# Second-layer expert weights laid out with two slots on the partitions, in a one-core ViT block with a soft mixture of experts

## What is computed

```python
y = jnp.einsum('btd,bst->bsd', xn, dispatch_w)          # 16 x 64 x 192
y = jnp.einsum('sio,bsi->bso', fc1_weight, y) + fc1_bias # 64 slots, 192 -> 768
y = jax.nn.gelu(y, approximate=False)
y = jnp.einsum('sio,bsi->bso', fc2_weight, y) + fc2_bias # 64 slots, 768 -> 192
out = jnp.einsum('bsd,bst->btd', y, combine_w)
```

## Time and profile before

| | |
|---|---|
| three executions | 221.20, 221.53, 221.94 us; median 221.53 |
| the profiled execution | 220.9 us |
| its span, first to last instruction | 219.1 us |
| busy: TensorE matmul / weight load / VectorE / ScalarE / GpSimd | 193.7 / 127.4 / 63.9 / 64.2 / 45.2 us |
| DMA | 80.68 MB in 17827 packets, mean 368 GB/s |
| packets under 8 KB | 13774 |

### The profile page before, as it was taken

One profiled execution on the slowest core, in us unless ns is written; L12 is line 12 of the kernel. 1 busy time (PEld: TensorE's weight loads), 2 busy tenths in 40 slices (PEclk: granted clock), 3 DMA queues, 4 the chain that ended last, 5 costly groups with the idle time before them and its releaser, 6 DMA issues.

```text
span 219.1 us, 4816 instructions
## 1 busy us (share of the span) xinstructions
PE 193.7 (88%) x2048; PEld 127.4 (58%) x2048; DVE 63.9 (29%) x153; ACT 64.2 (29%) x161; POOL 45.2 (21%) x91
## 2 busy tenths in 40 slices
PE   6699999999999998999999999839996789766994
PEld 6699876466667556556464655424564346532662
DVE  1556563579884631121110211100210011000213
ACT  2552433345565364150322304101300121010300
POOL 7701068575464400101001010100010000000000
PEclk9999999999999999999999999996999999997999
DMA  6999999999999499999999999999999999999912
GB/s 170 288 234 408 416 412 388 310 363 363 403 368 429 168 379 416 344 431 427 405 412 419 426 409 409 421 422 416 411 420 421 413 412 415 426 417 406 400 52 81
DMA packets 17827, 80.68 MB, mean 368 GB/s; under 512 B 2697, under 2 KB 4398, under 8 KB 13774
## 3 DMA queue, kind: packets, MB, share of 16 engines
q1 hardware_dynamic: 17806, 80.38, 94.6%
HBM read 79.46 MB, written 0.91 MB: 367 GB/s over the span
## 4 chain that ended last, share of the span: by engine, by line
DMA 48%; PE 41%; DVE 4%; ACT 2%; issue 2%; POOL 1%; SPq 0%; DVEq 0%; ACTq 0%; POOLq 0%
DMA ring<-in_L_ffn_fc_weight_dram 39%; PE ps L1285 9%; PE ps L1312 7%; PE ps L917 6%; PE ps L1259 4%; DMA value_store<-ring 3%; DMA ring<-value_store 3%; DMA ring<-in_x_dram 3%; PE ps L942 2%; PE ps L1137 2%; PE ps L1248 2%; PE ps L1298 2%; PE ps L911 1%; PE ps L1028 1%; PE ps L1041 1%
## 5 line engine op out<-in xcount | busy, mean ns | idle before, releaser
L1285 PE MATMUL ps<-ring,qkvT 128*32 128x384 f32 x384 | 43.4, 596 | 12.4 <-DMA ring<-in_L_ffn_fc_weight_dram 12.0
L1312 PE MATMUL ps<-ring,x_space 128*32 128x192 f32 x768 | 34.5, 328 | 4.3 <-DMA ring<-in_L_ffn_fc_weight_dram 3.6
L1285 PEld LDWEIGHTS ps<-ring,qkvT 128*32 128x32 f32 x384 | 12.9, 117 | 34.2 <-issue 28.6
L888 DVE TENSOR_TENSOR region_p<-ps,b1T 128x384 f32<-128x384 f32 x16 | 8.8, 557 | 81.4 <-PE ps L1298 81.4
L1312 PEld LDWEIGHTS ps<-ring,x_space 128*32 128x32 f32 x768 | 23.7, 110 | 14.3 <-DMA ring<-in_L_ffn_fc_weight_dram 5.3
L646 ACT ACTIVATE x_space<-ps,row_scale 128x384 f32<-128x384 f32 x16 | 15.1, 941 | 48.8 <-PE ps L1285 48.8
L1259 PE MATMUL ps<-projT,soft_space 128*108 128x192 f32 (+1 forms) x96 | 19.1, 329 | 0.4 <-ACT projT L683 0.4
L911 PEld LDWEIGHTS ps<-ident 128*128 128x128 f32 x116 | 15.5, 212 | 6.4 <-issue 4.6
L911 PE MATMUL ps<-ident 128*128 128x128 f32 x116 | 17.5, 304 | 1.8 <-POOL neg_half L384 1.8
L469 POOL COPY bias_space<-ident 64x128 f32<-64x128 f32 x8 | 2.2, 286 | 81.0 <-PE ps L1248 81.0
L683 ACT COPY projT<-ps 128x192 f32<-128x192 f32 x8 | 2.5, 318 | 52.7 <-PE ps L1312 52.7
(11 more groups left out here) (139 smaller groups left out, 218.3 us busy)
## 6 DMA issues: line engine op xcount, KB each, us to landing
ring<-in_L_ffn_fc_weight_dram SPq DMA_DIRECT2D x31, 2304.0 KB, 24.6
ring<-in_L_ffn_fc_weight_dram SPq DMA_DIRECT2D x3, 768.0 KB, 5.6
ring<-in_x_dram SPq DMA_DIRECT2D x2, 864.0 KB, 8.0
ring<-in_L_tok_W_proj_dram SPq DMA_DIRECT2D x1, 576.0 KB, 7.2
ring<-in_L_attn_w_qkv_dram SPq DMA_DIRECT2D x1, 432.0 KB, 10.6
out_dram<-h SPq DMA_DIRECT2D x2, 162.0 KB
value_store<-ring SPq DMA_DIRECT2D x1, 258.2 KB
ring<-value_store SPq DMA_DIRECT2D x3, 86.1 KB
```

The costliest lines, as they stand in the source:

```text
L888: dve.tensor_tensor(pre[:, pr, :, :].rearrange("p c (k b) -> p c k b", b=B), ps[:, 2 + pr, 0:384].rearrange("p (c k b) -> p c k b", c=3, b=B),
L1285: mm = pe.matmul(ps[32 * k:32 * k + 32, pr, 0:FF // 2], y_group[:, g % 2, j, 2 * pr + qq, :], w[:, qq, j, :, 3 * hf:3 * hf + 3], start=(j ...
L1312: mm = pe.matmul(ps[32 * q:32 * q + 32, 4, 0:D], gact[:, q // 2, k, 32 * l:32 * l + 32], w[:, q, c, :], start=(l == 0 and c == 0), stop=(l ...
```

## The change

Second-layer units take the layout of the first-layer ones. A unit now holds four *neighbouring* slots (two pairs q), and a partition holds twelve rows of 192 floats of one slot in one run of 9216 B: partitions 0 to 63 have the first slot of a pair (64 x 12 = 768 rows), 64 to 127 the second. To fit this, the hidden rows and the first bias must arrive with the slot's parity u on the partition half, so the three transposes of a turn become, for each of six column blocks, two matmuls against columns picked from the identity (`ident` seen as k, u, b), one into each half of the bank; the bias turn becomes 24 matmuls. GELU works on one half of the partitions with 384 elements. The second layer of unit 2 + l needs only the hidden rows of pair half l, and writes its own bank (4 or 3); its two column strips for even and odd c give two halves that are added: ScalarE copies one half (`keep_part`), VectorE adds the other (`fold`). `combine` waits for both. The first layer's moving columns are picked as 6 of 12 neighbouring floats instead of 3 of 6. The fillers write bank 2 instead of 3.

```diff
-        fc2_view = fc2_w.rearrange("(q l) (p c) d -> l p q (c d)", l=2, p=128)
+        fc2_view = fc2_w.rearrange("s f d -> (s f) d").rearrange("(q p c) d -> p q (c d)", p=128, c=2 * FC)
+        SECOND = (4, 3)
...
-                if u < 2:
-                    dst = ring[:, slot, :].rearrange("p (q n) -> p q n", q=2)
-                    src = fc1_view[:, 4 * g + 2 * u:4 * g + 2 * u + 2, :]
-                else:
-                    dst = ring[:, slot, :].rearrange("p (q n) -> p q n", q=4)
-                    src = fc2_view[u - 2][:, 4 * g:4 * g + 4, :]
-                sp.dma_start(dst, src).then_inc(unit_in[slot], 16)
+                pair = 4 * g + 2 * (u % 2)
+                src = (fc1_view if u < 2 else fc2_view)[:, pair:pair + 2, :]
+                sp.dma_start(ring[:, slot, :].rearrange("p (q n) -> p q n", q=2), src).then_inc(unit_in[slot], 16)
...
-                act.activation(gact[:, pr, :, :].rearrange("p k (l n) -> p k l n", l=2)[:, :, 0, 0:B],
-                               pre[:, pr, :, :].rearrange("p c (k l b) -> p (c k) l b", l=2, b=B)[:, :, 0, :],
-                               ACT.Gelu).then_inc(gact_ready, 1)
...
+                for u in range(2):
+                    half = slice(64 * u, 64 * u + 64)
+                    act.activation(gact[half, pr, :, B * u:B * u + B],
+                                   pre[half, pr, :, :].rearrange("p c (k b) -> p (c k) b", b=B),
+                                   ACT.Gelu).then_inc(gact_ready, 1)
+
+            def keep_part(g, l):
+
+                part = slice(64 * (1 - l), 64 * (1 - l) + 64)
+                act.wait_ge(units_used, g * UNITS + 3 + l)
+                act.copy(y2[64 * l:64 * l + 64, g % 2, :], ps[part, SECOND[l], 0:D]).then_inc(part_kept, 1)
...
-                act.wait_ge(units_used, (g + 1) * UNITS)
-                act.copy(y2[:, g % 2, :], ps[:, 4, 0:D]).then_inc(y2_ready, 1)
+                keep_part(g, 0)
+                keep_part(g, 1)
...
+            def fold(g, l):
+
+                part = slice(64 * l, 64 * l + 64)
+                dve.wait_ge(part_kept, 2 * g + l + 1)
+                dve.tensor_tensor(y2[part, g % 2, :], ps[part, SECOND[l], 0:D], y2[part, g % 2, :],
+                                  ALU.add).then_inc(y2_ready, 1)
...
+                fold(g, 0)
                 keep_mix(g, g % 2)
+                fold(g, 1)
...
-                b1v = b1_raw[0:S, :].rearrange("s (p c) -> s c p", c=FC)
-                for c in range(FC):
-                    mm = pe.transpose(ps[:, 3, c * S:(c + 1) * S], b1v[:, c, :], ident[0:S, 0:S])
+                b1v = b1_raw[0:S, :].rearrange("s (p c) -> s c p", c=2 * FC)
+                for c in range(2 * FC):
+                    for u in range(2):
+                        mm = pe.matmul(ps[64 * u:64 * u + 64, 3, c * S // 2:(c + 1) * S // 2], b1v[:, c, :],
+                                       ident[0:S, u:S:2], start=True, stop=True)
...
-                    pe.wait_ge(y2_ready, g + 1)
+                    pe.wait_ge(y2_ready, 2 * g + 2)
...
-                w = ring[:, slot, :].rearrange("p (q j n c) -> p q j n c", q=2, j=3, c=FC)
+                w = ring[:, slot, :].rearrange("p (q j n c) -> p q j n c", q=2, j=3, c=2 * FC)
...
-                                           w[:, qq, j, :, 3 * hf:3 * hf + 3],
+                                           w[:, qq, j, :, FC * hf:FC * hf + FC],
...
-                for c in range(3):
-                    mm = pe.transpose(ps[:, 2 + pr, c * 128:(c + 1) * 128], hid[:, pr, c, :], ident[:, :])
+                for c in range(FC):
+                    for u in range(2):
+                        mm = pe.matmul(ps[64 * u:64 * u + 64, 2 + pr, c * 64:(c + 1) * 64], hid[:, pr, c, :],
+                                       ident[:, :].rearrange("p (k u b) -> p u k b", u=2, b=B)[:, u, :, :],
+                                       start=True, stop=True)
...
-                if l == 0:
-                    pe.wait_ge(gact_ready, g * 4 + 4)
-                    earlier(pe, y2_ready, g)
...
+                pe.wait_ge(gact_ready, g * 4 + 2 * l + 2)
+                earlier(pe, y2_ready, 2 * g)
+                w = ring[:, slot, :].rearrange("p (q c d) -> p q c d", q=2, c=2 * FC)
+                for c in range(2 * FC):
+                    for q in range(2):
+                        k = 2 * (c % 2) + q
+                        mm = pe.matmul(ps[32 * k:32 * k + 32, SECOND[l], 0:D],
+                                       gact[:, l, (c % FC) * 4 + 2 * q + c // FC, :], w[:, q, c, :],
+                                       start=(c < 2), stop=(c >= 2 * FC - 2), tile_position=(0, 32 * k))
```

More of the change, by code:

```diff
@@ L667, in _ @@
                     for hf in range(2):
-                        act.copy(b1T[:, :, :, 2 * hf:2 * hf + 2],
-                                 ps[:, 3, hf * 3 * S:(hf + 1) * 3 * S].rearrange("p (c q l) -> p c q l", c=3, l=2)
-                                 ).then_inc(b1_kept, 1)
+                        act.copy(b1T[:, :, :, hf], ps[:, 3, hf * 3 * S:(hf + 1) * 3 * S]
+                                 .rearrange("p (c q) -> p c q", c=6)).then_inc(b1_kept, 1)
                 keep_hidden(g, 1)
@@ L1304, in second_layer @@
                 pe.wait_ge(unit_in[slot], 16 * ((g * UNITS + 2 + l) // RING) + 16)
-                if l == 0:
-                    pe.wait_ge(gact_ready, g * 4 + 4)
-                    earlier(pe, y2_ready, g)
-                w = ring[:, slot, :].rearrange("p (q c d) -> p q c d", q=4, c=FC)
-                for c in range(FC):
-                    for q in range(4):
-                        k = (c % 3) * 4 + 2 * (q % 2) + c // 3
-                        mm = pe.matmul(ps[32 * q:32 * q + 32, 4, 0:D], gact[:, q // 2, k, 32 * l:32 * l + 32],
-                                       w[:, q, c, :], start=(l == 0 and c == 0), stop=(l == 1 and c == FC - 1),
-                                       tile_position=(0, 32 * q))
+                pe.wait_ge(gact_ready, g * 4 + 2 * l + 2)
[7 more added lines that the diff above has]
+                                       start=(c < 2), stop=(c >= 2 * FC - 2), tile_position=(0, 32 * k))
                 mm.then_inc(units_used, 1)
```

27 lines of the change are left out of this document (12 added, 15 removed).

## The result

| | before | after |
|---|---|---|
| median of 10 executions each | 221.88 us | 223.94 us (222.77 to 226.34) |
| ratio after / before | | 1.0081, interval 1.0045 to 1.0117 |
| the profiled execution | 220.9 us | 225.61 us |
| its span | 219.1 us | 223.9 us |
| DMA packets | 17827 | 13734 |

The profiled execution of after lies 1.7 us above its median.

A forecast was written before the change was run, and what follows sets the result against it. DMA and TensorE were taken to share the end. Unit 2 +0.3 us and eleven late units -1.65 made the last landing -1.35; with the addition's +0.4, -0.95 us: 220.6 us on the median, 8 in 10 from 219.7 to 222.4.

The forecast's parts named there:

- What bounds the kernel: DMA and TensorE both set the end, unit 31's start at 210.95 us; either one alone becoming earlier wins nothing.
- Long runs: Second-layer loads in 9216 B runs: 0.15 us less for each of 11 late units, -1.65 us.
- the early part: Two second-layer units with long runs, ahead of the stored values and their reload: -0.3 us from 44 us on.
- Bias turn: Ahead of unit 2: 24 pairs at 70 ns, 1.68 us instead of 0.89, +0.79 us (+0.57 to +1.34).
- unit 10's issue: Early in the weight queue: this issue moves by +0.03 us and stays hidden.
- rival A: Unit 29 again at 1.2 GHz, TensorE ends last, the DMA's gain is wasted: +0.1 us, 221.6 us; chance 0.22.
- Hidden turns: Each turn of hidden rows, now 12 pairs at 70 ns: 0.84 us instead of 0.38, +0.46 us.
- rival B: In the turns, the two array halves run one after the other: +2.8 us, 224.3 us; chance 0.06, milder form 0.08.
- First layer: Moving rows read in 24 B runs: gain of 0 to 0.46 us a unit, half taken, 0.23.
- Rival D: First layer unchanged, so unit 2 is 0.46 us later: -0.5 us, 221.0 us; chance 0.12.
- TensorE at the end: From unit 29's landing at 198.5 us, TensorE at full clock is free at 209.1, before unit 31's landing.
- Fold: After the last unit, VectorE's addition of the two halves lies on the path: +0.4 us.

The follow-up runs named there:

- e7: After, with the first bias gathered beforehand by GpSimd into neighbouring floats and without the last group's fillers ahead of unit 31: 221.55 us, ratio to before 0.9948.
- e10: After, with the first bias gathered beforehand by GpSimd into neighbouring floats, all fillers kept: 221.74 us, ratio to before 0.9946.
- e1: Before, with only the second-layer loads changed to runs of 9216 B (weights in wrong order, same work): 219.93 us, ratio to before 0.9914.
- e6: After, with 26 filler instructions instead of 10 ahead of unit 29 in the last group: median 226.27 us.
- e9: Before, with second-layer loads in 9216 B runs and first-layer columns picked as 6 of 12 floats: 219.60 us, ratio to before 0.9885.
- e3: After, with the bias turn's 48 instructions reading neighbouring floats (wrong bias values, same work): 222.47 us in one execution.
- e2: After, with the bias turn as in before, six transposes (bias values in wrong places): 220.26 us, ratio to before 0.9924.
- e8: Before, with only the first layer's moving columns picked as 6 of 12 floats instead of 3 of 6: 220.34 us in one execution.
- e11: After, with the first bias gathered by GpSimd and hidden rows turned by three transposes again (wrong row order): 220.85 us, ratio to before 0.9946.
- e5: After, without the ten filler instructions ahead of unit 31 in the last group: 223.67 us, ratio to before 1.0023.
- e4: After, with the bias turn moved ahead of the values' matmuls: 228.05 us, ratio to before 1.0025.

## Why the prediction was wrong

**The sum against the profiled execution.** Unit 31 was forecast for 209.6 and started at 215.30, 5.7 us later. Up to unit 2 that is 3.4 us, in the main 1.7 from the bias turn (3.35 us instead of 1.68), 2.1 because the first unit started 1.83 us late instead of 0.3 early, and -0.5 because the first layer gained its whole 0.96. From unit 2 to the landing of unit 31 it is another 1.0, and 1.25 is TensorE coming behind that landing. The bias turn is the part that the change brings and that the experiments remove: with it at 1.52 us, near its forecast price, e7 and e10 lie 1.2 us below before, where the forecast was 0.95.

**What bounds the kernel.** Right in part: both bounds are close together at the end, but "if either one alone becomes earlier, nothing is won" isn't so. e1 changed nothing but the loads, and unit 31 started 1.28 us earlier, since unit 29's shorter wait left it the full clock. Unit 31 has no DMA wait in after, 1.54 us in e7 and 0.26 in e6.

**Long runs.** Right in mechanism: 1.65 + 0.3 had been predicted, and e1 alone gave 1.9. That the size fits so well is in part luck. The 0.3 for the early part isn't borne out (e9), and in the profiles e1 wins only 0.93 us between unit 2 (84.65) and unit 31 (209.67), where before has 85.00 and 210.95. The Trainium skill, page "DMA: Bandwidth & Descriptors", section "Why small descriptors are slow", would make the gain 1% by the estimate in the prediction; the trace has 2% (411 to 420 GB/s), so it doesn't agree here.

**Bias turn.** This is the step that failed. I priced its 24 pairs at 70 ns, from rows whose weights lie side by side, and carried "may cost more" only as an upper end of +1.34 us. It measured +2.46: 3.35 us, 140 ns a pair. e3 shows that neighbouring floats bring it to 63 ns, e2 that the old six transposes bring the time to 0.9924. The earlier trace rows had a price that comes near. The old bias turn, which read its weights 24 B apart, took 0.89 us for 6 x 128 weight columns, 1.16 ns a column. The new one loads 24 x 128 = 3072 columns (each pair reads its 64 columns twice, once for each half), which makes 3.6 us at that price. I divided the row by the wrong thing: by instructions, to see how many there would be, instead of by columns read. Even so that row could not have told that the distance is what costs: the hidden turn of the earlier trace rows, whose columns lie side by side, took 0.38 us for 3 x 128 columns, 0.99 ns a column. The distance as the cause is shown by e3 and by the gathered bias.

The Trainium skill, page "SBUF — State Buffer", section "Specifications (TRN2)", says that a 16-byte line needs two hits or more for full bandwidth. I had used that rule for the first layer alone. It speaks of any read, and the weights of the bias turn get one hit a line. e3 and e8 agree with it in direction, 63 against 140 ns and 2.07 against 2.55 us.

**Where the delay goes.** I had unit 10's issue moved by 0.03 us and hidden. With the bias turn at its real price, unit 1 ends 3.3 us later. Unit 10's issue is no longer hidden, and the queue runs dry a second time: 346 GB/s over 80 to 96 us in after and 349 in e6, against 394 in before, 395 in e10 and 413 in e2. The 1.8 us of the queue lost there are about the bias turn's excess. The whole kernels differ by more: after lies 3.5 us above e2, whose turn is 2.46 us shorter, and 3.0 above e10, whose turn is 1.8 shorter. Both excesses, 1.0 and 1.2 us, are as large as the uncertainty. What the rest would be, if there is one, isn't shown; rival A and the clock at 70 us are candidates.

**Hidden turns.** Right: 0.85 us measured (206.61 to 207.46) for 0.84 predicted, 70 ns a pair. Two ahead of unit 2 with the activation make +0.33 us (10.19 in e2 less 9.86 in e9), where 0.46 - 0.18 = 0.28 had been predicted. The halves do overlap; rival B fell.

**First layer.** Half of 0.46 had been taken, and the whole came: 2.55 to 2.07. Rival D fell, and the rule of that page of the Trainium skill gave the right size. It is the one term of the sum that was too pessimistic.

**TensorE at the end.** Rival A, which I gave 0.22, is what the profile shows: unit 29 at the low clock (3.72 us), 12.34 us from its start to unit 31, and no wait there. I argued against it that waits of that size don't always cost the clock. That is true and was no reason to set the case aside. With about 2.0 us of idle time ahead of unit 29, the profiles of before, after, e2, e3, e9 and e11 have the low clock and those of e5 and e7 the full one. In after's profile A cost 1.25 us of its own: unit 31 would otherwise have started at its landing, at about 214.05, as it did in e6 and e7 11.09 and 11.07 us behind unit 29. The forecast that unit 31 starts after a DMA wait failed here. What A costs in the median isn't shown, since the clock of unit 29 isn't known for executions without a profile. A alone doesn't make the kernel slower than before: e2 has it in its profile (3.81 us, no wait ahead of unit 31) and a ratio of 0.9924.

**Fold.** Right: +0.4 predicted, 0.39 measured.

**Not foreseen.** The clock of 0.50 at 70 to 72 us, worth about 1.3 us in the profiled execution. It came in e10 as well (0.67 at 69 to 71 us and 0.50 at 71 to 73), which still beat before. It isn't in the profiles of before and of the other ten experiments. How often it comes in after is open, and so is why most executions of e4 and e6 took 3 to 6 us more than their profiled ones.

## What to carry to other kernels

Price a matmul that reads its weights at a distance by the columns that it loads and the time of one such column in the nearest row that reads at a distance, not by the number of instructions. Before adding work that runs only once, look which issues hang on its end: here 2.5 us in the first of eight groups emptied a queue that was busy from there to its end, and undid what the 11 late units with long runs had won. And gathering on an idle engine (1.5 us on GpSimd at 17 us) gave back what 48 spread reads had cost on the critical one.

## What the runs showed of the hardware

- A pair of weight loads of 64 f32 columns with 32 moving columns takes 63 ns when the columns lie side by side and 140 ns when they lie 48 B apart: 1.1 ns for each column read.
- Moving rows read in runs of 12 B take 2.55 us where runs of 24 B take 2.07, for the same 24 instructions of 384 columns. 24 B is as fast as contiguous (2.09 us for as many columns in the second layer).
- 9216 B runs move at 418 to 423 GB/s, 4608 B runs at 410 to 413.
- The low clock is not tied to the length of the wait ahead of it: after 2.0 us of idle time the same unit ran in 2.14 us in two kernels and in 3.7 to 3.9 in six, and after 2.81 us in 2.14 (e10). After waits of 0.2 to 0.4 us it kept the full clock in all four kernels that had them (e1, e4, e6, e8).
